# Another order of PSUM banks for the eight expansion matmuls of a slot-attention output pass

## The chip, the cores and the metric

The kernel runs on all 8 cores of one Trainium2 chip. Each core computes one element of the batch (8192 rows of 1024 numbers); the cores don't exchange anything. The metric is the device time of the slowest core in microseconds, as the median over several executions of the program.

## The reference

The input `x` is (8, 8192, 1024) in float32. The output adds two branches to it, both computed from the row-normalised `xn`:

```python
xn = _layernorm(x, axis=-1)
x = x + _L0_attn_ref(xn, ...) + _L0_ffn_ref(xn, ...)
```

The first branch is a gated recurrence over the 8192 rows, with three projections of `xn` before it and one after it (`y @ Wo + bo`). The second sends every row to its 8 best of 64 slots, collects the slots over all rows of the sequence, updates them (a recurrent cell, attention among the 64 slots, a layer norm, a projection), and gives each row its share of the slots back:

```python
slot_input = jnp.einsum('bts,btd->bsd', alpha, x)   # needs every row
...
slot_values = y @ wvp + bvp                          # 64 x 1024
out = jnp.einsum('bts,bsd->btd', alpha, slot_values)
return out @ wo + bo
```

The slots need every row before any row of the second branch's output can be made. So the rows are gone through twice.

## The kernel before

**Stages.** The kernel has three stages on each core, with the rows in 16 phases of `Tp` = 512. Pass 1 (`wo_block`, `slot_pe`, `xn_transposes`, `h_logits`, `wku_loop`, for each phase) computes the recurrence and its output, writes `x` plus the first branch to `out`, keeps the routing weights of all rows in the tile `alpha_T` (64 x 8192), and adds the slots up. The middle stage updates the 64 slots and ends in `sv_bf` (64 x 1024), the slot values. Pass 2 is what the change touches: for each phase it reads 2 MB of `out` back, adds the second branch, and writes 2 MB.

**One phase of pass 2.** Its parts are these. First the read of `out` into `prd` (L1015), one DMA of 2048 KB issued by SP. Then `zmm_phase(p2 + 1)`, which makes the expansion `z` of the next phase: for k = 0 to 7 one matmul of 64 rows by 512 columns (L992, `sv_bf` by `alpha_T`) into one bank of PSUM, which ScalarE copies as bf16 into `z_f` (L1000). Then four output tiles i = 0 to 3 of 128 rows by 1024, each 16 matmuls of 128x512 (L1031, `z_f` of this phase by `wo2_sb`) and two matmuls for the bias (L1038) into a pair of banks. VectorE adds each tile's banks to `prd` (L1046), and SP writes the tiles in two stores of 1024 KB (L1053), after the second and the fourth addition. `z_f` and `prd` have two buffers, used in turn.

**Banks.** Six banks are used, in three tensors of two: A0 and A1 in `psA`, B0 and B1 in `psB`, C0 and C1 in `psC`. The output tiles 0 to 3 use A, B, C and A again. The expansion matmul k uses `zregs[k]`. The helper `pe_claim(bank)` makes PE wait for the event that last released this bank: for an output tile that is the VectorE addition (`fadd`), for an expansion matmul it is the ScalarE copy (`zev`).

**What sets the order.** Every engine runs its own instructions in the order in which `build_walk` lists them, and waits at semaphores. PE therefore runs, for each phase: the eight expansion matmuls of the next phase, then tiles 0, 1, 2, 3. Before the first phase there are two groups of eight (`zmm_phase(0)`, `zmm_phase(1)`); the last phase, p2 = 15, has none. SP issues the read of phase p2 behind the second store of phase p2 - 1, so behind that phase's last addition. In phase p2's tile 0 VectorE waits for the read of this phase as well.

Of the kernel before, what the change touches and what calls it, by code (L numbers as in the profile page):

```python
# [104 lines left out]
def build_walk(cfg, t, P):  # L105
# [872 lines left out]
    release("A0", ("sv",))  # L978
    release("A1", ("sv",))

    zregs = ["A0", "A1", "B0", "B1", "C0", "C1", "A0", "A1"]

    def zmm_phase(q):
        if q == 0:
# [106 lines left out]
def build_nc(cfg):  # L1091
# [70 lines left out]
    with ExitStack() as ctx:  # L1162
# [121 lines left out]
        with ExitStack() as pctx:  # L1284
# [8 lines left out]
            P = Plan()  # L1293
            P.begin("dry")
            build_walk(cfg, t, P)

            with nc.Block() as block:
                @block.sync
                def _(eng):
                    P.begin("sy", eng, sems)  # L1300
                    build_walk(cfg, t, P)

                @block.gpsimd
                def _(eng):
                    P.begin("gp", eng, sems)
                    build_walk(cfg, t, P)

                @block.tensor
                def _(eng):
                    P.begin("pe", eng, sems)  # L1310
                    build_walk(cfg, t, P)

                @block.vector
                def _(eng):
                    P.begin("ve", eng, sems)
                    build_walk(cfg, t, P)

                @block.scalar
                def _(eng):
                    P.begin("se", eng, sems)  # L1320
                    build_walk(cfg, t, P)
# [73 lines left out]
```

How the kernel before makes its waits and increments, by code:

```python
    def dma(self, engine, fn, pool, event=None):  # L76
        eng_of, k = DMA_POOLS[pool]
        assert eng_of == engine
        i = self.pool_n[pool]
        self.pool_n[pool] = i + 1
        sem = f"{pool}{i % k}"
        if i >= k and self.mode == engine:
            self.eng.wait_ge(self.sems[sem], 16 * (i // k))
        return self.op(engine, fn, inc=sem, inc_n=16, event=event)
# [1 line left out]
    def wait(self, engine, event):  # L86
        if self.mode == engine:
            sem_name, val, _ = self.events[event]
            self.eng.wait_ge(self.sems[sem_name], val)
# [1 line left out]
    def wait_all_dma(self, engine, event, pool):  # L91
        if self.mode == engine:
            _, _, snap = self.events[event]
            _, k = DMA_POOLS[pool]
            for i in range(k):
                sem = f"{pool}{i}"
                if snap.get(sem, 0) > 0:
                    self.eng.wait_ge(self.sems[sem], snap[sem])
# [6 lines left out]
def build_walk(cfg, t, P):  # L105
# [972 lines left out]
        P.dma("sy", lambda s: s.dma_start(out=t.o_xnf[:], in_=t.xn_f[:]), "so")  # L1078
        P.dma("sy", lambda s: s.dma_start(out=t.o_ysbf[:], in_=t.ys_bf[:]), "so")
        P.dma("sy", lambda s: s.dma_start(out=t.o_lsb[:], in_=t.l_sb[:]), "so")
    if P.mode == "sy":
        _, k = DMA_POOLS["so"]
        n = P.pool_n["so"]
        for i in range(k):
            cnt = 16 * ((n - i - 1) // k + 1) if n > i else 0
            if cnt:
                P.eng.wait_ge(P.sems[f"so{i}"], cnt)
```

## Time and profile before

| | |
|---|---|
| median of 3 runs | 1904.35 us (1903.08 to 2004.16) |
| the profiled execution | 1903.06 us |
| span of its slowest core, core 5 | 1901.4 us |
| spans of the 8 cores | 1884.7 to 1901.4 us |
| matmul busy on core 5 | 1539.0 us of the span |
| VectorE, ScalarE busy on core 5 | 751.6 us, 569.7 us |
| pass 2 on core 5, from the first expansion matmul | from 1502.5 us to the end |
| read of `out`, from issue to landing (median) | 9.8 us |
| stores of pass 2, from issue to landing (median) | 4.9 us |

All the views below are of core 5 unless a line says otherwise, and times are counted from the start of its span. "Idle before" is the time in which an engine did nothing, and the arrow names what it waited for last. A matmul of 512 columns has a record of some 0.38 us but the next begins after 0.22 us when the granted clock is full, since they overlap; at half the clock the next begins after 0.43 us.

### The profile page before, as it was taken

How to read it: one execution, taken by the hardware profiler on the slowest of the kernel's cores; microseconds unless marked ns; L12 is line 12 of the kernel's file. 1: busy time of each engine (PE TensorE's matmuls, PEld its weight loads, DVE VectorE, ACT ScalarE, POOL GpSimd, SP SyncE). 2: the span in 40 equal slices, each digit the busy share in tenths (PEclk: the TensorE clock that was granted, in tenths of full speed). 3: DMA queues.
4: the chain of work that ended last, by engine and by line, in shares of the span. 5: the costliest groups of instructions: out<-in, count | busy, mean ns of one | idle time of the engine just before them, and what ended most of it. 6: DMA issues, size and time to landing. Idle time of an engine off the chain costs nothing.

```text
span 1901.4 us, 20893 instructions; the slowest of 8 cores (1884.7 to 1901.4 us)
## 1 busy us (share of the span) xinstructions
PE 1539.0 (81%) x7221; PEld 672.6 (35%) x7221; DVE 751.6 (40%) x1359; ACT 569.7 (30%) x926; POOL 26.6 (1%) x54
## 2 busy tenths in 40 slices
PE   0078989889899898998988989989543488888888
PEld 0034434444444443444444444444211133333332
DVE  0036446464564554635646446364302021222222
ACT  0142515325244252352532525332002111111110
POOL 0100000000000000000000000000110000000000
PEclk9999989999999999999999999999766688888888
DMA  9802020220202202112022020210596344444445
GB/s 155 179 4 75 15 89 1 89 69 21 89 13 77 89 1 89 39 51 89 1 89 60 30 89 1 89 45 1 123 170 110 89 177 177 169 158 163 164 166 199
DMA packets 42679, 166.52 MB, mean 88 GB/s; under 512 B 4290, under 2 KB 5458, under 8 KB 41682
## 3 DMA queue, kind: packets, MB, share of 16 engines
q1 hardware_dynamic: 36178, 134.29, 20.8%
q0 software_dynamic: 6400, 30.89, 9.9%
q8 instruction: 62, 1.02, 0.2%
q14 instruction: 39, 0.32, 0.1%
HBM read 128.68 MB, written 67.11 MB: 103 GB/s over the span
## 4 chain that ended last, share of the span: by engine, by line
PE 69%; DMA 10%; DVE 9%; issue 5%; ACT 4%; DVEq 3%; another core or an unknown queue 1%; ACTq 0%; POOL 0%; POOLq 0%; SPq 0%
PE psA L1031 8%; PE psA L485 6%; PE psA L489 6%; PE psC L494 6%; PE psB L494 6%; PE psC L489 6%; PE psB L485 6%; PE psA L555 4%; PE psA L347 3%; PE psC L1031 3%; PE psB L1031 3%; PE psB L555 3%; DVEq L102 3%; DMA sb_Wu_sb<-Wu_pk 2%; ACT sb_z_f L1000 2%
## 5 line engine op out<-in xcount | busy, mean ns | idle before, releaser
L19 ACT ACT_TABLE_LOAD x83 | 106.5, 1283 | 394.3 <-PE psA L555 376.6
L525 DVE SCALAR_TENSOR_TENSOR sb_a_sb<-sb_g_sb,sb_s_sb 128x512 f32<-128x512 f32 x128 | 88.7, 693 | 293.7 <-ACT sb_s_sb L510 293.7
L1031 PE MATMUL psA<-sb_wo_sb,sb_z_f 128*128 128x512 bf16 x512 | 146.5, 450 | 35.0 <-ACT sb_z_f L1000 33.3
L537 DVE TENSOR_TENSOR_SCAN sb_ys_bf<-sb_a_sb,sb_ys_bf,sb_b_sb 128x512 bf16<-128x512 f32 x120 | 154.1, 1284 | 9.7 <-issue 0.9
L347 PE MATMUL psA<-sb_Wo_sb,sb_ys_bf 128*128 128x512 bf16 x512 | 121.6, 387 | 27.2 <-DVE sb_x_sl L375 27.2
L1046 DVE TENSOR_TENSOR sb_prd<-psA,sb_prd 128x1024 f32<-128x1024 f32 x32 | 39.2, 1225 | 255.9 <-PE psA L1038 209.8
L1000 ACT ACTIVATE sb_z_f<-psA 128x512 bf16<-128x512 f32 x64 | 35.8, 631 | 307.6 <-PE psA L992 307.6
L485 PE MATMUL psA<-sb_xn_f,sb_Wp_sb 128*128 128x512 bf16 x512 | 122.5, 383 | 0.0
L489 PE MATMUL psA<-sb_xn_f,sb_Wp_sb 128*128 128x512 bf16 x512 | 121.2, 380 | 0.0
L489 PE MATMUL psC<-sb_xn_f,sb_Wp_sb 128*128 128x512 bf16 x512 | 121.0, 379 | 0.0
L485 PE MATMUL psB<-sb_xn_f,sb_Wp_sb 128*128 128x512 bf16 x512 | 120.9, 379 | 0.0
L494 PE MATMUL psB<-sb_xn_f,sb_Wu_sb 128*128 128x512 bf16 x512 | 120.9, 379 | 0.0
L494 PE MATMUL psC<-sb_xn_f,sb_Wu_sb 128*128 128x512 bf16 x512 | 120.9, 379 | 0.0
L1031 PEld LDWEIGHTS psA<-sb_wo_sb,sb_z_f 128*128 128x128 bf16 x512 | 54.7, 112 | 128.5 <-issue 93.4
L508 ACT ACTIVATE sb_g_sb<-psA,sb_bpw 128x512 f32<-128x512 f32 x64 | 44.1, 689 | 171.4 <-PE psB L494 167.5
L555 PE MATMUL psA<-sb_xn_f,sb_w1t_sb 128*128 128x512 bf16 x256 | 83.4, 497 | 12.9 <-DVE sb_xn_f L469 12.9
L460 PE MATMUL psT<-sb_ident,sb_xn_tm 128*128 128x128 bf16 x512 | 53.3, 243 | 48.1 <-DVE sb_alpha_T L425 24.0
L594 DVE MAX8 sb_m<-sb_l_sb 128x8 f32<-128x64 f32 x64 | 9.7, 213 | 195.9 <-ACT sb_l_sb L588 195.9
L508 ACT ACTIVATE sb_g_sb<-psB,sb_bpw 128x512 f32<-128x512 f32 x64 | 44.1, 689 | 130.6 <-PE psC L494 116.6
L347 PEld LDWEIGHTS psA<-sb_Wo_sb,sb_ys_bf 128*128 128x128 bf16 x512 | 49.8, 99 | 93.6 <-issue 38.6
L489 PEld LDWEIGHTS psA<-sb_xn_f,sb_Wp_sb 128*128 128x128 bf16 x512 | 50.2, 98 | 61.0 <-issue 1.0
L494 PEld LDWEIGHTS psB<-sb_xn_f,sb_Wu_sb 128*128 128x128 bf16 x512 | 50.1, 98 | 60.4
(224 smaller groups left out, 1899.9 us busy)
## 6 DMA issues: line engine op xcount, KB each, us to landing
sb_x_sl<-x SPq DMA_DIRECT2D x32, 1024.0 KB, 8.2
out<-sb_x_sl SPq DMA_DIRECT2D x32, 1024.0 KB, 4.1
sb_prd<-out SPq DMA_DIRECT2D x16, 2048.0 KB, 9.8
out<-sb_prd SPq DMA_DIRECT2D x32, 1024.0 KB, 4.9
sb_WT<-Wih_pk POOLq DMA_DIRECT2D x12, 512.0 KB, 8.7
sb_whh_pp<-Whh_pk POOLq DMA_DIRECT2D x12, 512.0 KB, 8.5
sb_Wp_sb<-Wp_pk POOLq DMA_DIRECT2D x1, 4096.0 KB, 30.4
sb_Wu_sb<-Wu_pk POOLq DMA_DIRECT2D x1, 2048.0 KB, 41.3
```

The costliest lines, as they stand in the source:

```text
L19: return eng.add_instruction(mybir.InstLoadActFuncSet(name=eng.bass.get_next_instruction_name(), act_func_set_id=idx, ins=[], outs=[]))
L102: self.eng.drain()
L347: P.op("pe", lambda e, i=i, f=f, k=k, ps=ps: e.matmul(ps[:, f * 512:(f + 1) * 512], t.ys_bf[:, k, i * 128:(i + 1) * 128], t.Wo_sb[:, k, f ...
L485: P.op("pe", lambda e, j=j, k=k, psw=psw: e.matmul(psw, t.Wp_sb[:, k, j * 128:(j + 1) * 128], t.xn_f[:, k, :], start=(k == 0), stop=(k == ...
L489: P.op("pe", lambda e, j=j, k=k, psk=psk: e.matmul(psk, t.Wp_sb[:, k, 1024 + j * 128:1024 + (j + 1) * 128], t.xn_f[:, k, :], start=(k == 0 ...
L494: P.op("pe", lambda e, j=j, k=k, psu=psu: e.matmul(psu, t.Wu_sb[:, k, j * 128:(j + 1) * 128], t.xn_f[:, k, :], start=(k == 0), stop=(k == ...
L508: P.op("se", lambda s, j=j, psw=psw: s.activation(t.g_sb[:, j % 2, :], psw, AF.Sigmoid, bias=t.bpw[:, j:j + 1]))
L525: P.op("ve", lambda v, pp=pp: v.scalar_tensor_tensor(t.a_sb[:], t.g_sb[:, pp, :], -2.0, t.s2_sb[:, pp, :], ALU.mult, ALU.mult))
L537: P.op("ve", lambda v, j=j, init=init: v.tensor_tensor_scan(t.ys_bf[:, j, :], t.a_sb[:], t.b_sb[:], init, ALU.mult, ALU.add), inc="sve", e ...
L555: P.op("pe", lambda e, jh=jh, k=k, ps=ps: e.matmul(ps, t.w1t_sb[:, k, jh * 128:(jh + 1) * 128], t.xn_f[:, k, :], start=(k == 0), stop=(k = ...
L1000: P.op("se", lambda s, k=k, q=q, ps=ps: s.activation(t.z_f[:, q % 2, k, :], ps, AF.Identity), inc="sse", event=("zev", q, k))
L1031: P.op("pe", lambda e, i=i, f=f, k=k, ps=ps, p2=p2: e.matmul(ps[:, f * 512:(f + 1) * 512], t.z_f[:, p2 % 2, k, i * 128:(i + 1) * 128], t.w ...
```

## The change

One list is replaced: the banks that the eight expansion matmuls of `zmm_phase` take in turn. Matmuls 0 and 1 go to C0 and C1 instead of A0 and A1, matmuls 4 and 5 to A0 and A1 instead of C0 and C1, and matmuls 6 and 7 to C0 and C1 instead of A0 and A1. Matmuls 2 and 3 stay in B0 and B1. The number of instructions, their order on every engine, the sizes and the DMAs are the same. Only which release each `pe_claim` waits for changes.

```diff
-    zregs = ["A0", "A1", "B0", "B1", "C0", "C1", "A0", "A1"]
+    zregs = ["C0", "C1", "B0", "B1", "A0", "A1", "C0", "C1"]
```

## Rows read from the trace of the kernel before

**Rows 1.** The page: the span in 40 slices, PE busy and granted PE clock, in tenths
```profile
PE   0078989889899898998988989989543488888888
PEclk9999989999999999999999999999766688888888
```
**Rows 2.** Chain that ended last, 1600 to 1680 us: start, duration, what
```profile
1653.26 0.55 PE psA L1038 x2
...
1653.90 1.24 DVE sb_prd L1046
...
1655.27 0.59 PE psA L992 x2
...
1660.12 4.99 PE psA L1031 x16
...
1665.64 3.56 PE psB L1031 x16
```
**Rows 3.** Timeline, 1640 to 1695 us: start, duration, engine, what, count, idle before
```profile
1649.64 3.63 PE L1031 MATMUL psA<-sb_wo_sb,sb_z_f 128*128 128x512 bf16 x16
1653.20 0.60 PE L1038 MATMUL psA<-sb_bo_tot,sb_ones_r 1*128 1x512 bf16 x2
1655.27 0.59 PE L992 MATMUL psA<-sb_alpha_T,sb_sv_bf 64*128 64x512 bf16 x2 [1.48 <-DVE sb_prd L1046]
1655.83 0.38 SPq L1015 DMA_DIRECT2D sb_prd<-out  x1
1655.83 1.09 ACT L1000 ACTIVATE sb_z_f<-psA 128x512 bf16<-128x512 f32 x2 [20.32 <-PE psA L992]
1657.76 1.12 ACT L1000 ACTIVATE sb_z_f<-psC 128x512 bf16<-128x512 f32 x2
1658.72 1.15 ACT L1000 ACTIVATE sb_z_f<-psA 128x512 bf16<-128x512 f32 x2
1660.12 4.99 PE L1031 MATMUL psA<-sb_wo_sb,sb_z_f 128*128 128x512 bf16 x16 [2.07 <-ACT sb_z_f L1000]
```
**Rows 4.** Waits, 1502 to 1902 us: engine and line, releaser, us, times, longest
```profile
DVE sb_prd L1046 <- DMA sb_prd<-out: 46.2, 4, 11.7
PE psA L1031 <- ACT sb_z_f L1000: 33.3, 15, 2.7
PE psA L992 <- DVE sb_prd L1046: 20.7, 14, 1.5
```
**Rows 5.** Timeline: the first and the last tile 0 of pass 2
```profile
1511.80 5.75 PE L1031 MATMUL psA<-sb_wo_sb,sb_z_f 128*128 128x512 bf16 x16 [1.33 <-ACT sb_z_f L1000]
1877.61 5.30 PE L1031 MATMUL psA<-sb_wo_sb,sb_z_f 128*128 128x512 bf16 x16 [1.69 <-DVE sb_prd L1046]
```
**Rows 6.** Groups by line, 1502 to 1902 us: busy us, mean ns, idle before
```profile
L1031 PE MATMUL psA<-sb_wo_sb,sb_z_f 128*128 128x512 bf16 x512 | 146.5, 450 | 35.0 <-ACT sb_z_f L1000 33.3 <-DVE sb_prd L1046 1.7
L1031 PE MATMUL psB<-sb_wo_sb,sb_z_f 128*128 128x512 bf16 x256 | 58.0, 380 | 0.0
```
**Rows 7.** Stretches: length, busy PE, PEld, DVE, ACT, POOL, PEclk, DMA share, GB/s
```profile
1656.00:1656.50 0.50, 0.50 (x3) 0.16 (x2) 0.00 (x0) 0.50 (x2) 0.00 (x0) 0.62 0.81 336
...
1662.50:1663.00 0.50, 0.50 (x2) 0.15 (x1) 0.00 (x0) 0.00 (x0) 0.00 (x0) 0.56 0.91 360
```
**Rows 8.** The same columns: two kinds of PE gap in pass 1, each twice
```profile
173.00:177.00 4.00, 2.30 (x12) 0.91 (x11) 4.00 (x7) 0.00 (x0) 0.00 (x0) 1.00 0.03 14
251.00:257.00 6.00, 3.88 (x11) 1.36 (x11) 4.25 (x8) 0.00 (x0) 0.00 (x0) 0.72 0.31 128
181.00:192.00 11.00, 7.54 (x43) 3.65 (x41) 4.76 (x12) 0.62 (x1) 0.00 (x0) 0.69 0.90 279
498.00:509.00 11.00, 7.59 (x52) 4.05 (x53) 4.33 (x12) 2.66 (x3) 0.00 (x0) 1.00 0.93 276
```
**Rows 9.** The reads of line 1015, to landing: on core 5, then on core 0
```profile
DMA to landing us min/median/max: 9.3/9.8/20.3
DMA to landing us min/median/max: 10.1/10.6/17.9
```

## The prediction

> **What bounds the kernel now.** I read the views in the order of the groups. In the strip of the page [rows 1], passes and middle stage can be told apart: PE is busy at 8 or 9 tenths in most slices up to slice 28, falls to 3 in the middle stage, and is at 8 again from slice 33. The clock line is what the reader should notice: 9 in pass 1, 8 in pass 2. So something in pass 2 makes PE lose its clock again and again.
>
> The chain of waits [rows 2] shows what. PE's bias matmuls of the last tile end, then comes a VectorE addition of 1.24 us, then the first expansion matmuls, and then ScalarE copies up to 1660.12, where tile 0 begins. Everything else in the chain is PE. The waits [rows 4] show that this is a pattern: expansion matmul 0 waits for an addition 14 times (20.7 us, 1.48 each), and tile 0 waits for ScalarE 15 times (33.3 us). The 14 are phases 1 to 14; phase 0 has nothing before it and phase 15 has no expansion. The first and the last tile 0 [rows 5] give the mean length of a phase: (1877.61 - 1511.80) / 15 = 24.39 us.
>
> So pass 2 is bound by PE and, between two phases, by a gap in which VectorE and ScalarE are the path. DMA isn't: VectorE waits for the read of `out` in 4 phases [rows 4], but this doesn't reach PE, which works on tile 1 meanwhile.
>
> **The gap before.** I take the one at 1653 [rows 3]. The bias pair begins at 1653.20; such a pair keeps PE for 0.53 us (tile 0 ends at 1660.12 + 4.99 = 1665.11 and tile 1 starts at 1665.64, with a pair between them [rows 2]), so PE is free at 1653.73. Tile 3's addition releases A0 and A1 and matmul 0 starts at 1655.27. ScalarE starts 0.56 us later, at 1655.83, and its eight copies end at 1658.72 + 1.15 = 1659.87. Tile 0 starts 0.25 us after that, at 1660.12. The gap is 6.39 us. Matmuls 6 and 7, on A0 and A1, are copied last, and tile 0 needs exactly these banks: it waits for all eight copies.
>
> **The change, part by part.**
>
> 1. *Matmuls 0 and 1 on C0 and C1.* These were released by tile 2's addition, which runs during tile 3, so matmul 0 follows the bias pair at 1653.73 and not at 1655.27: the copies start 1.54 us earlier, at 1654.29. Matmuls 2 and 3 (B0, B1) follow at once. ScalarE's other wait there, that `z_f`'s buffer is free, is for the end of tile 3, which is past.
> 2. *Matmuls 4 and 5 on A0 and A1.* They now bear the wait for tile 3's addition and start at 1655.27, ready for ScalarE at 1655.83. Queued behind them on PE are matmuls 6 and 7 and tile 0, which is late anyway. ScalarE comes to its fifth copy at 1654.29 + (1657.76 - 1655.83) = 1656.22. The cover is 0.39 us, so this wait costs nothing; if the cover goes, the cost is the excess.
> 3. *Matmuls 6 and 7 on C0 and C1.* They need copies 0 and 1, long done. Tile 0 needs only the sixth copy, which ends at 1657.76 + 1.12 = 1658.88 in the old timing, 0.99 us before the eighth. Copies 7 and 8 run beside tile 0; tile 2 wants their banks some 8 us later.
>
> Sum for one gap: 1.54 + 0.99 = 2.53 us. Tile 0 starts at 1657.59 and the gap is 3.86 us. Over 14 gaps this is 35.4 us. At the start of pass 2, where sixteen copies run in a row, only the 0.99 counts. Phase 15 keeps its wait for tile 3's addition (1.69 us) [rows 5]. Together 36.4 us.
>
> 4. *The clock.* In the gap of the rows the granted clock fell to 0.50, the 1.2 GHz level, at about 1656.1 and was back at 2.4 GHz at about 1662.9 [rows 7]. The part in tile 0, 2.8 us at half speed, costs 1.4 us: tile 0 took 4.99 us, a full-speed tile 3.56 [rows 2]. Over pass 2, `psA` is busy 146.5 us in 32 tiles, and `psB` 58.0 in 16, or 3.63 each [rows 6]: 146.5 - 32 x 3.63 = 30.3 us are lost to the slow clock in 16 tiles 0, some 1.9 each. The clock fell in every one of the 15 gaps.
>
> Does it still fall in a gap of 3.86 us? In it PE's records would show two pauses, about 0.5 us ahead of matmul 4 and 1.3 us ahead of tile 0, against 1.48 and 2.07 now [rows 3]. Pass 1 has the nearest gaps [rows 8]. A single pause of 1.70 us before a tile (the stretch at 173) left the clock at 1.00, one of 2.12 us (at 251) didn't; it fell at 2 of 15 such places. The stretch with transposes, PE busy 7.5 of 11 us, ended either way: 0.69 at 181, 1.00 at 498, with a fall at 11 of 15 boundaries. The new gap lies between the two kinds, so I take a fall in half of the gaps, 7 of 14. When it falls, more of the slow stretch lies in tile 0, since tile 0 begins 2.53 us earlier: (1662.9 - 1657.59) / 2 = 2.7 us a fall. That is 7 x 2.7 = 18.9 us where 14 x 1.9 = 26.6 were: 7.7 us back. Bounds: no fall gives 26.6 back; a fall in every gap costs 14 x 2.7 - 26.6 = 11.2 more.
>
> The Trainium skill ("TensorE: Matmul & The Clock Gate", section "Why this matters for your kernels") warns only of longer pauses between bursts than any of the two in this gap, before or after. By that rule the clock would stay up and the whole 26.6 us would come back; but it speaks against the trace, where pauses as short as 1.48 and 2.07 us lost it 15 times of 15, so it is a rival and not the forecast.
>
> 5. *The read of `out`.* It is issued 0.7 us after the last addition (1655.83 against 1653.90 + 1.24), as now, and lands 9.8 us later, at 1665.6; on core 0 it takes 10.6 [rows 9]. Tile 0's banks are ready at 1665.6 now and will be at 1657.59 + 3.56 + 0.53 = 1661.7, or 1664.4 with a slow clock, so VectorE will wait for the read in nearly every phase. PE does not, until tile 3 wants A0 and A1. The loop is: issue 0.7, landing L, addition 1.23, release 0.13, tile 3 up to its addition 1653.90 - 1649.64 = 4.26, addition 1.23: L + 7.6 us. With L = 9.8 it is 17.4, with 10.6 it is 18.2, against a phase of 24.39 - 2.53 - 1.9 = 19.96 us even if no clock is lost. It costs nothing until L passes 12.3.
>
> **Sum.** 36.4 + 7.7 = 44.1 us off the profiled execution's 1903.06 gives 1859. The median of the runs is 1.3 us above that execution; I leave the forecast at 1859, against 1904.35.
>
> **The rivals.**
>
> - *The clock never falls* (the page's rule): 36.4 + 26.6 = 63 us, 1840. For it: the single pauses of 1.7 us that left it up. Against: the expansion matmuls fill only part of the gap and use half of the rows.
> - *The clock falls in every gap*: 36.4 - 11.2 = 25 us, 1878. For it: 15 of 15 now. Against: the gap shrinks from 6.39 to 3.86 us and each pause with it.
> - *The read becomes the bound.* Phases are shorter, so the same 4 MB come more often, and the other cores ask more often too. At L = 15 a phase is 22.6 us: (24.39 - 22.6) x 14 = 25 us, 1878. Against it: the medians of L are 9.8 and 10.6 now, the lowest 9.3 and 10.1 [rows 9], so the bulk is near the bottom.
> - *Slower than before*, by the same loop: only once L + 7.6 passes 24.39, at L over 16.8. At L = 18 a phase is 25.6 us, 14 x 1.2 = 17 us more, 1920. One read did take 20.3 us [rows 9], but the median says that the others don't come near.
> - *The order of banks does nothing*, since the copies turn out to be held by something else: 1903. Against: ScalarE's idle time ahead of the copies ends with the matmul [rows 3].
>
> **How the numbers follow.** Forecast 0.60 (its own range 1850 to 1869), clock never falls 0.13, clock always falls 0.14, read as the bound 0.06, no effect 0.04, slower 0.03. The likeliest gives 1859. For 8 in 10 I reach most of the way to the two clock cases: 1842 to 1877. About 2% is what a measurement of this kernel can tell from no change; 2% faster is 1866. The forecast's range lies below that with 0.55 of its 0.60; with 0.13 for the clock that stays and 0.03 of the read's case, faster has 0.71. The rest of the forecast, the clock that always falls, no effect and the rest of the read's case give 0.25 for within 2%. Slower has 0.04.
>
> **What would show it.** In the waits, the one of an expansion matmul for the addition stays 14 times but falls from 1.48 to about 0.5 us, and lies behind the first four matmuls. Tile 0 starts about 3.9 us after the bias pair. The wait of tile 0 for ScalarE falls from 33.3 us to some 20. The read is what ends VectorE's wait in nearly all phases, with no wait of tile 3's matmuls for it. The busy time of `psA` falls from 146.5 to about 139 us. Pass 1 and the middle stage don't change. I am wrong if tile 3 waits for VectorE, if ScalarE stands idle ahead of its fifth copy, or if the slow clock takes much more or less than half of the gaps.

## The result and the profile after

The changed kernel takes 1858.36 us in the median of 8 runs, the kernel before 1903.29 us in the runs beside them. The ratio is 0.9771, with a 95% interval of 0.9759 to 0.9784: faster by 2.3%, 44.9 us. The forecast was 1859. In some executions, whatever the kernel, the cores of one die show a lower granted clock and take some per cent longer; ratios compare the others alone, and the four kernels whose ratio would have a wide interval or none (`e9_spread_ahead`, `e10_early_fill`, `e11_six_fill`, `e12_readahead`) are read by the phase lengths in their traces.

The spans of the profiled execution (1861.40 us) are 1844.0 to 1859.9 us over the eight cores; the slowest is again core 5. All that follows is of core 5 unless it says otherwise. First the timeline around one gap, where [rows 3] showed the same of before (start, duration, engine, what, count, idle before):

```profile
1639.22 0.60 PE L1038 MATMUL psA<-sb_bo_tot,sb_ones_r 1*128 1x512 bf16 x2
1639.75 0.60 PE L992 MATMUL psC<-sb_alpha_T,sb_sv_bf 64*128 64x512 bf16 x2
1639.93 1.22 DVE L1046 TENSOR_TENSOR sb_prd<-psA,sb_prd 128x1024 f32<-128x1024 f32 x1 [2.87 <-PE psA L1038]
1640.20 0.59 PE L992 MATMUL psB<-sb_alpha_T,sb_sv_bf 64*128 64x512 bf16 x2
1640.33 1.08 ACT L1000 ACTIVATE sb_z_f<-psC 128x512 bf16<-128x512 f32 x2 [16.20 <-PE psC L992]
1641.30 0.59 PE L992 MATMUL psA<-sb_alpha_T,sb_sv_bf 64*128 64x512 bf16 x2 [0.51 <-DVE sb_prd L1046]
...
1642.25 1.12 ACT L1000 ACTIVATE sb_z_f<-psA 128x512 bf16<-128x512 f32 x2
1643.21 1.14 ACT L1000 ACTIVATE sb_z_f<-psC 128x512 bf16<-128x512 f32 x2
...
1643.67 6.26 PE L1031 MATMUL psA<-sb_wo_sb,sb_z_f 128*128 128x512 bf16 x16 [1.35 <-ACT sb_z_f L1000]
```

The reader is to see three things. The expansion matmul on C0 follows the bias pair at once, 0.53 us after its start, ahead of VectorE's addition and not behind it. The wait for that addition has moved to the matmul on A0 at 1641.30 and is 0.51 us long. And tile 0 starts at 1643.67, while ScalarE is still at copies 7 and 8 (1643.21 + 1.14 = 1644.35). From 1639.75, when the bias pair frees PE, the gap is 3.92 us; it was 6.39. Over the 14 gaps of core 5 the mean is 3.88 us; it was 6.41.

The waits of pass 2 (engine and line, releaser, us, times, longest) against [rows 4]:

```profile
DVE sb_prd L1046 <- DMA sb_prd<-out: 163.7, 15, 11.9
...
PE psA L1031 <- ACT sb_z_f L1000: 18.6, 15, 1.4
```

And the groups by line (busy us, mean ns, idle before) against [rows 6]:

```profile
L1031 PE MATMUL psA<-sb_wo_sb,sb_z_f 128*128 128x512 bf16 x512 | 140.7, 437 | 20.3 <-ACT sb_z_f L1000 18.6 <-DVE sb_prd L1046 1.7
L992 PE MATMUL psA<-sb_alpha_T,sb_sv_bf 64*128 64x512 bf16 x32 | 10.3, 404 | 7.2 <-DVE sb_prd L1046 7.2
```

VectorE now waits for the read of `out` in 15 phases, not 4, and none of this reaches PE: tiles 1 to 3 have no idle time in front of them. PE's wait for VectorE ahead of the expansion fell from 20.7 us to 7.2 us, tile 0's wait for ScalarE from 33.3 to 18.6, and the busy time of `psA` from 146.5 to 140.7. That last one is the clock. Three tiles 0 in a row, from the timeline:

```profile
1643.67 6.26 PE L1031 MATMUL psA<-sb_wo_sb,sb_z_f 128*128 128x512 bf16 x16 [1.35 <-ACT sb_z_f L1000]
...
1666.54 5.08 PE L1031 MATMUL psA<-sb_wo_sb,sb_z_f 128*128 128x512 bf16 x16 [1.30 <-ACT sb_z_f L1000]
...
1688.24 3.61 PE L1031 MATMUL psA<-sb_wo_sb,sb_z_f 128*128 128x512 bf16 x16 [1.30 <-ACT sb_z_f L1000]
```

The record of a tile at full clock is 3.61 to 3.63 us long. So one tile 0 lost 2.6 us, the next 1.4 and the third nothing, behind the same gap of 3.9 us. This pattern of three repeats through most of pass 2. On core 5, 10 of the 14 tiles 0 behind a changed gap lost time, 20.8 us together, and 4 did not; on the other cores 8 to 10 of 14 did. Before, it was 14 of 14, and 26.6 us.

### The profile page after: what moved, and what is told of

Its sections match the earlier page's. It is cut to its first block, busy times and chain, and to the rows that moved or that the text cites. A ratio compares the mean times of both kernels' runs of the same rounds, so it can differ in the third digit from the quotient of the medians.

```text
span 1859.9 us, 20893 instructions; the slowest of 8 cores (1844.0 to 1859.9 us)
## 1 busy us (share of the span) xinstructions
PE 1520.4 (82%) x7221; PEld 668.2 (36%) x7221; DVE 751.2 (40%) x1359; ACT 568.6 (31%) x926; POOL 26.6 (1%) x54
## 4 chain that ended last, share of the span: by engine, by line
PE 69%; DMA 10%; DVE 9%; issue 5%; DVEq 3%; ACT 2%; another core or an unknown queue 1%; ACTq 0%; POOL 0%; POOLq 0%; SPq 0%
PE psA L1031 8%; PE psA L485 6%; PE psC L494 6%; PE psA L489 6%; PE psC L489 6%; PE psB L494 6%; PE psB L485 6%; PE psA L555 4%; PE psA L347 3%; PE psC L1031 3%; PE psB L1031 3%; PE psB L555 3%; DVEq L102 3%; DMA sb_Wu_sb<-Wu_pk 2%; DMA sb_WT<-Wih_pk 2%
## 5 line engine op out<-in xcount | busy, mean ns | idle before, releaser
L1031 PE MATMUL psA<-sb_wo_sb,sb_z_f 128*128 128x512 bf16 x512 | 140.7, 437 | 20.3 <-ACT sb_z_f L1000 18.6
L1046 DVE TENSOR_TENSOR sb_prd<-psA,sb_prd 128x1024 f32<-128x1024 f32 x32 | 39.2, 1225 | 249.6 <-DMA sb_prd<-out 163.7
L1000 ACT ACTIVATE sb_z_f<-psC 128x512 bf16<-128x512 f32 x64 | 35.6, 627 | 268.7 <-PE psC L992 268.7
L494 PEld LDWEIGHTS psC<-sb_xn_f,sb_Wu_sb 128*128 128x128 bf16 x512 | 50.1, 98 | 60.4
## 6 DMA issues: line engine op xcount, KB each, us to landing
sb_prd<-out SPq DMA_DIRECT2D x16, 2048.0 KB, 10.6
sb_Wu_sb<-Wu_pk POOLq DMA_DIRECT2D x1, 2048.0 KB, 41.6
```

Source lines behind the costliest of these rows:

```text
L494: P.op("pe", lambda e, j=j, k=k, psu=psu: e.matmul(psu, t.Wu_sb[:, k, j * 128:(j + 1) * 128], t.xn_f[:, k, :], start=(k == 0), stop=(k == ...
L1031: P.op("pe", lambda e, i=i, f=f, k=k, ps=ps, p2=p2: e.matmul(ps[:, f * 512:(f + 1) * 512], t.z_f[:, p2 % 2, k, i * 128:(i + 1) * 128], t.w ...
```

## The experiments

All of them are edits of pass 2. Where a phase length is given, it is the distance between the same instruction in successive phases, in the steady part of pass 2.

### The two parts of the change, each alone

`e1_early` keeps the early start but puts A0 and A1 last, so tile 0 still needs all eight copies. `e2_six` keeps the late start but has A0 and A1 at places 4 and 5, so tile 0 needs six.

```diff
-    zregs = ["C0", "C1", "B0", "B1", "A0", "A1", "C0", "C1"]
+    zregs = ["C0", "C1", "B0", "B1", "C0", "C1", "A0", "A1"]   # e1_early
+    zregs = ["A0", "A1", "B0", "B1", "A0", "A1", "C0", "C1"]   # e2_six
```

> Banks C0 C1 B0 B1 C0 C1 A0 A1: only the start of the copies moves, tile 0 still needs all eight copies. Theory (two additive parts, 1.54 and 0.99 us a gap): the gap from the bias pair to tile 0 is 6.4 - 1.5 = 4.9 us; 14 x 1.54 = 21.6 us off, of which the slow clock takes some 5 us back since it still falls in most gaps: about 1886. Rival (the early start is all of the gain, the copies 7 and 8 are hidden anyway): as the changed kernel, 1858.

> Banks A0 A1 B0 B1 A0 A1 C0 C1: the first matmul still waits for the last addition, but tile 0 needs only six copies. Theory: the gap is 6.4 - 1.0 = 5.4 us; 15 x 0.99 = 15 us off, some 5 taken back by the slow clock, which falls in every gap: about 1893. Rival (tile 0 is held by PE's own order and not by the copies): no change, 1903.

Measured: `e1_early` has a ratio to before of 0.9947 (0.9930 to 0.9964), about 10 us faster; `e2_six` 0.9930 (0.9909 to 0.9952), about 13 us. I expected 17 and 10. One by one the two parts give 10 + 13 = 23 us, and together 44.9. The timeline of `e1_early`, core 2:

```profile
1655.40 6.29 PE L1031 MATMUL psA<-sb_wo_sb,sb_z_f 128*128 128x512 bf16 x16 [2.24 <-ACT sb_z_f L1000]
...
1679.29 6.30 PE L1031 MATMUL psA<-sb_wo_sb,sb_z_f 128*128 128x512 bf16 x16 [2.24 <-ACT sb_z_f L1000]
```

A phase is 23.89 us. The bias pair before the second of these tiles 0 ends at 1674.44, where the expansion begins, so the gap is 4.85 us, 1.54 shorter than before, as expected. But the 14 tiles 0 of this core now take 6.1 to 6.3 us each, where they took 5.0 to 6.5. `psA` is busy for 155.4 us, against 146.5 before: the slow clock took 9 us of the 21.6 back. In `e2_six` the gap is 5.41 us, 0.98 shorter than before, and the phases settle at 23.9 us as well, with 2.1 us lost in each tile 0 (core 2):

```profile
1671.30 5.74 PE L1031 MATMUL psA<-sb_wo_sb,sb_z_f 128*128 128x512 bf16 x16 [0.63 <-ACT sb_z_f L1000]
...
1695.19 5.75 PE L1031 MATMUL psA<-sb_wo_sb,sb_z_f 128*128 128x512 bf16 x16 [0.63 <-ACT sb_z_f L1000]
```

So the gap of each kernel is the one expected, and my charge of 5 us for the clock was too small in `e1_early`. Gap and loss add up to the same in both, 4.85 + 2.7 and 5.41 + 2.1 us, so the clock came back at the same place behind the bias pair. Why it did, no run here tells.

### The same with the clock held up

To take the clock out, PE gets idle work in its pauses: transposes of the identity into a PSUM bank that nobody reads in pass 2. `e3_fill_new` does this on the changed kernel, `e4_fill_old` on the kernel before, `e10_early_fill` and `e11_six_fill` on the two halves.

```diff
+    def fill(n):
+        for _ in range(n):
+            P.op("pe", lambda e: e.transpose(t.psT0[:, 0:128], t.ident[:], t.ident[:]))
...
+            if q >= 2 and k == 4:
+                fill(8)          # old banks: 22 ahead of k == 0
             pe_claim(reg)
...
+        if q >= 2:
+            fill(20)             # old banks: 42
```

> The changed kernel plus idle work for PE in its two pauses: 8 transposes of 128x128 ahead of expansion matmul 4 and 20 behind matmul 7, in 14 phases, into a bank that nobody reads. Theory: the granted clock stays at 1.00 through the gaps, the busy time of psA falls from 140.7 to about 119, and the kernel gains some 22 us: 1836. The gap itself keeps its 3.9 us. Rival (the fall doesn't depend on PE's work in the gap, or the transposes don't hold the clock): 1858 or, if they push tile 0 back, up to 10 us more.

> The kernel before plus the same idle work in its pauses: 22 transposes ahead of matmul 0, 42 behind matmul 7, in 14 phases. Theory: the clock stays up, psA's busy time falls from 146.5 to about 119, 28 us off: 1875. With the run of the changed kernel with idle work this gives the effect of the order of banks at a constant clock, 14 x 2.53 + 1 = 36 us. Rival (order and clock can't be told apart, the bank order works by the clock alone): both runs with idle work give the same time.

> Banks C0 C1 B0 B1 C0 C1 A0 A1 (early start, eight copies) plus idle work for PE in the pauses: 6 transposes ahead of matmul 4, 38 behind matmul 7. Theory (the two parts of the change add up at a constant clock, and only the slow clock ate the single ones): a phase is 22.74 - 1.54 = 21.2 us, and 14 x 1.54 = 21.6 us come off the old banks with idle work: ratio to before about 0.974. Rival (the parts need each other): 22.5 us a phase or more.

> Banks A0 A1 B0 B1 A0 A1 C0 C1 (late start, six copies) plus idle work: 22 transposes ahead of matmul 0, 6 ahead of matmul 4, 20 behind matmul 7. Theory: a phase is 22.74 - 0.99 = 21.75 us, 15 us off the old banks with idle work: ratio to before about 0.978. Rival as above: 22.5 us a phase or more.

Measured: `e3_fill_new` 0.9672 (0.9654 to 0.9689), `e4_fill_old` 0.9855 (0.9834 to 0.9876). The stretch of pass 2 in both (length, busy PE, PEld, DVE, ACT, POOL, granted clock, DMA share, GB/s), first the new banks (core 1), then the old ones (core 4):

```profile
1510.00:1840.00 330.00, 317.11 (x1657) 133.94 (x1656) 76.04 (x64) 57.53 (x115) 0.00 (x0) 0.99 0.59 198
```
```profile
1510.00:1870.00 360.00, 348.01 (x2160) 163.42 (x2160) 78.28 (x64) 57.26 (x114) 0.00 (x0) 0.99 0.50 179
```

The granted clock is 0.99 in both, where the kernel before has 0.85 and the changed kernel 0.91 over the same stage (core 5, in this order):

```profile
1512.00:1901.00 389.00, 329.04 (x1264) 120.52 (x1262) 78.31 (x64) 56.44 (x112) 0.00 (x0) 0.85 0.45 168
```
```profile
1512.00:1860.00 348.00, 315.03 (x1264) 117.05 (x1261) 77.83 (x64) 56.54 (x113) 0.00 (x0) 0.91 0.56 187
```

`psA` is busy 117.6 and 119.4 us in the two kernels with idle work. By ratio they take 1841 and 1876 us; I expected 1836 and 1875. Both expectations of the theory hold: the clock follows what PE does in the gap, and the order of banks has a worth of its own. Between the two, 0.9855 - 0.9672 = 0.0183 of 1902 us is 35 us, against the 36.4 of the sum.

The timelines give it per phase, since on nearly all cores each phase of these kernels behind the first is as long as the next. Core 1 of `e3_fill_new` is an exception, with four phases that are 0.3 to 0.6 us longer; there the read of `out` takes 12.0 us in the median, and tile 3 has to wait for VectorE. The bias pairs of tile 3 follow each other in `e4_fill_old` (core 4) by 22.74 us and in `e3_fill_new` (core 1) by 20.23 us:

```profile
1665.31 0.60 PE L1049 MATMUL psA<-sb_bo_tot,sb_ones_r 1*128 1x512 bf16 x2
...
1688.05 0.60 PE L1049 MATMUL psA<-sb_bo_tot,sb_ones_r 1*128 1x512 bf16 x2
```
```profile
1650.17 0.60 PE L1049 MATMUL psA<-sb_bo_tot,sb_ones_r 1*128 1x512 bf16 x2
...
1670.40 0.60 PE L1049 MATMUL psA<-sb_bo_tot,sb_ones_r 1*128 1x512 bf16 x2
...
1708.19 3.61 PE L1042 MATMUL psA<-sb_wo_sb,sb_z_f 128*128 128x512 bf16 x16 [0.53 <-DVE sb_prd L1057]
```

The halves, `e10_early_fill` (core 0) first and `e11_six_fill` (core 0) second, by the starts of tile 3:

```profile
1652.83 3.63 PE L1042 MATMUL psA<-sb_wo_sb,sb_z_f 128*128 128x512 bf16 x16
...
1674.04 3.63 PE L1042 MATMUL psA<-sb_wo_sb,sb_z_f 128*128 128x512 bf16 x16
```
```profile
1649.86 3.63 PE L1042 MATMUL psA<-sb_wo_sb,sb_z_f 128*128 128x512 bf16 x16
...
1671.62 3.63 PE L1042 MATMUL psA<-sb_wo_sb,sb_z_f 128*128 128x512 bf16 x16
```

| banks, clock held up | phase, us | shorter by | the sum said |
|---|---|---|---|
| old | 22.74 | | |
| early start, eight copies | 21.21 | 1.53 | 1.54 |
| late start, six copies | 21.76 | 0.98 | 0.99 |
| both, the change | 20.23 | 2.51 | 2.53 |

At a constant clock the two parts add up. Only the slow clock makes them look as though they needed each other. The ratio of `e10_early_fill`, 0.974 as expected, has a wide interval (0.958 to 0.990), and `e11_six_fill` has none; the phase lengths carry this reading.

### A shorter chain still

`e5_four` gives A0 and A1 to matmuls 2 and 3, so tile 0 needs only four copies.

```diff
-    zregs = ["C0", "C1", "B0", "B1", "A0", "A1", "C0", "C1"]
+    zregs = ["C0", "C1", "A0", "A1", "B0", "B1", "C0", "C1"]
```

> Banks C0 C1 A0 A1 B0 B1 C0 C1: tile 0 needs only four copies, but matmul 2 is now the one that waits for the last addition. Theory: matmul 2 starts 1.54 us behind the bias pair, its copy 0.56 later at 2.1 us, which is 0.5 us after the second copy could end, so ScalarE stands idle once; copies 3 and 4 end at 3.2 us and tile 0 starts at 3.45 us, against 3.92 in the changed kernel. 14 x 0.47 = 7 us off and a little more by the clock: 1850. Rival (the cover of the matmul that waits was already used up, so a shorter chain gives nothing): 1858 or slower.

Measured: 0.9751 (0.9736 to 0.9766), against 0.9771 for the change; in time some 4 us less, and the intervals overlap. Core 6:

```profile
1679.18 0.59 PE L992 MATMUL psA<-sb_alpha_T,sb_sv_bf 64*128 64x512 bf16 x2 [0.94 <-DVE sb_prd L1046]
...
1680.99 5.22 PE L1031 MATMUL psA<-sb_wo_sb,sb_z_f 128*128 128x512 bf16 x16 [0.35 <-ACT sb_z_f L1000]
```

The expansion began at 1677.63, so this gap is 3.36 us where I expected 3.45. ScalarE does stand idle once, ahead of its third copy:

```profile
1679.65 1.09 ACT L1000 ACTIVATE sb_z_f<-psA 128x512 bf16<-128x512 f32 x2 [0.36 <-PE psA L992]
```

But in 11 to 13 of the 14 gaps a tile 0 still lost time to the clock, more often than in the change, whose gap is longer. The pause in the middle is longer (0.94 against 0.51 us) and the one ahead of tile 0 shorter (0.35 against 1.35). The losses are smaller on average than in the change, and their sum is about the same: 16 to 23 us a core against 17 to 21. Nor are all the gaps 3.36 us; some are 3.7 to 4.2, and the mean of a core is 3.46 to 3.66 us, where the change has 3.87 to 4.04. By the gap shown 14 x (3.92 - 3.36) = 7.8 us were to be had; about half of it came. The longer gaps took part of the rest, and the clock, which I had expected to add to the gain, added nothing.

### When the read of `out` is late

Two kernels queue one more read ahead of each read of `out`, of 2 MB and of 4 MB, into a buffer that nobody reads.

```diff
+        if p2 >= 1:
+            P.dma("sy", lambda s, p2=p2: s.dma_start(
+                out=t.xtra[:, 0:4, :],   # 4 MB: 0:8, from (p2 - 1) * Tp
+                in_=t.i_x[p2 * Tp:p2 * Tp + 4 * 128, :]...), "sx")
```

> The changed kernel with one more read of 2 MB (of x, into a buffer nobody reads) queued ahead of each read of out in phases 1 to 15. Theory (a phase can't be shorter than L + 7.6 us, L the time from the issue of the extra read to the landing of the read of out): L becomes 14.5 to 16, the bound 22 to 23.6 against a mean phase of 21.6; 15 x (0.5 to 2) = 8 to 30 us slower than the changed kernel: 1866 to 1888. Tile 3 then waits for VectorE. Rival (the read is hidden anyway, VectorE's wait never reaches PE): 1858.

> The same with an extra read of 4 MB. Theory: L is 20 to 22 us, a phase 27.6 to 29.6, 15 x 6 to 15 x 8 = 90 to 120 us slower than the changed kernel: 1948 to 1978, the last addition's wait for A0 and A1 in the chain of each phase. Rival (the read is hidden): 1858. This is the mechanism by which the change could have been slower than before.

Measured: 1.0127 (1.0095 to 1.0159) and 1.0718 (1.0684 to 1.0752), so (1.0127 - 0.9771) x 1903 = 68 us and likewise 180 us more than the changed kernel. Direction and place are right, the size is not: I expected 8 to 30 and 90 to 120. The read of `out` lands 16.6 us after its issue in the first kernel (median, core 4) and 22.7 us in the second (core 6):

```profile
DMA to landing us min/median/max: 14.0/16.6/21.2
DMA to landing us min/median/max: 20.0/22.7/24.3
```

This gives L + 7.6 = 24.2 and 30.3, but the phases of these cores are 26.5 and 33.1 us long. The timeline of the second shows what the formula left out:

```profile
1645.92 0.60 PE L1043 MATMUL psC<-sb_bo_tot,sb_ones_r 1*128 1x512 bf16 x2
1655.44 6.11 PE L1036 MATMUL psA<-sb_wo_sb,sb_z_f 128*128 128x512 bf16 x16 [8.92 <-DVE sb_prd L1051]
1661.49 0.60 PE L1043 MATMUL psA<-sb_bo_tot,sb_ones_r 1*128 1x512 bf16 x2
```

Tile 3 waits 8.92 us for the addition that frees A0 and A1, and then runs 6.11 us and not 3.63: the wait costs the clock too, in the very loop that is the bound. The loss is 2.5 us here, 1.3 to 2.9 and in the mean 2.2 us over the phases of this core, and 1.9 in the mean on core 4 of the first kernel. With it, 30.3 + 2.2 = 32.5 and 24.2 + 1.9 = 26.1 us; the 0.4 to 0.6 us that are left stay open. The rest of the expectation holds: the read reaches PE through tile 3's banks and through nothing else (139.6 us of waits of `psA` for the addition, in 15 phases).

The other direction, the changed kernel with the read of phase p2 + 1 issued ahead of the stores of phase p2:

```diff
-        P.dma("sy", ... out=t.prd[:, pr, :, :] ..., event=("pread", p2))
+        if p2 == 0:
+            pread(0)
+        if p2 + 1 < NPH:
+            pread(p2 + 1)
```

> The changed kernel with the read of out issued one phase earlier and nothing else. VectorE's waits for the read (163.7 us in 15 phases) should vanish. Theory (they never reached PE, since the loop through the read is 3 us or so shorter than a phase): same time as the changed kernel, 1858, ratio 0.977. Rival (the read was on the path in some phases): 1850 or less.

Measured: mostly phases of 20.2, 21.7 and 22.9 us as in the changed kernel, a mean of 21.4 to 21.8 us on the cores (21.5 to 21.9 there), and times from 1856.89 us; the ratio, 0.9733, has a wide interval (0.9610 to 0.9857) that holds the changed kernel's. VectorE's waits for the read are gone from the trace, 163.7 us of them on the changed kernel's core 5, and nothing was gained. They were beside the path.

### No gap at all

`e8_spread` issues the expansion in pairs behind the output tiles, in the two banks of the transposes, and lets the output tiles take A, B and C in turn across phases. `e9_spread_ahead` adds the early read.

```diff
+        trio = [("A0", "A1", t.psA), ("B0", "B1", t.psB), ("C0", "C1", t.psC)]
+        oregs = [trio[(4 * p2 + i) % 3] for i in range(4)]
...
             release(r1, ("fadd", p2, i))
+            if p2 + 1 < NPH:
+                zmm_phase(p2 + 1, (2 * i, 2 * i + 1))
```

> No gap at all: the eight expansion matmuls of the next phase are issued in pairs behind the output tiles 0 to 3 and use the two PSUM banks of the transposes (free in pass 2), and the output tiles take A, B and C in turn through all phases. Theory: a phase is 4 x 4.09 + 8 x 0.22 = 18.1 us of PE's work with the clock at 1.00, if the read allows it: L + 7.6 with L = 10 to 11 gives 17.6 to 18.6. 15 x (21.6 - 18.4) = 48 us off the changed kernel and some 5 at the start: about 1806. Rival (PE isn't the bound once the gap is gone, since copies and additions share the banks' ports or the read is late): 1825 or more, with PE idle ahead of tile 3.

> The spread kernel with the read of out issued one phase earlier: SP issues the read of phase p2 + 1 ahead of the stores of phase p2, so it has a whole phase to land. Theory (what lengthened single phases of the spread kernel from 18.5 to 19 or 21 us was a late read that held tile 3): every phase is 18.5 us (4 x (4.09 + 0.53)) on every core, and the kernel gains another 5 to 15 us: about 1808. Rival (the long phases come from elsewhere, and the read ahead only meets the stores): no change, 1820, or slower.

Measured: `e8_spread` 0.9623 (0.9604 to 0.9643), 1816.33 us at best, with spans of 1799.2 to 1814.8. It is the fastest kernel with a ratio, but it is not as fast as expected: 0.9623 x 1903 is 1831 us, and I had said 1806. The timeline on core 3:

```profile
1648.96 3.63 PE L1029 MATMUL psA<-sb_wo_sb,sb_z_f 128*128 128x512 bf16 x16
1652.52 0.60 PE L1036 MATMUL psA<-sb_bo_tot,sb_ones_r 1*128 1x512 bf16 x2
1653.05 0.60 PE L992 MATMUL psT<-sb_alpha_T,sb_sv_bf 64*128 64x512 bf16 x2
1653.59 3.63 PE L1029 MATMUL psB<-sb_wo_sb,sb_z_f 128*128 128x512 bf16 x16
```

There is no idle time of PE left in such a phase, the granted clock of this core is 1.00 over pass 2, and the pair costs 0.53 us, not 2 x 0.22 as I expected: 4 x (4.09 + 0.53) = 18.5 us, which is the phase length. But single phases took 19 to 21.7 us. On core 5:

```profile
1720.86 5.30 PE L1029 MATMUL psC<-sb_wo_sb,sb_z_f 128*128 128x512 bf16 x16 [1.26 <-DVE sb_prd L1044]
...
1741.62 3.61 PE L1029 MATMUL psA<-sb_wo_sb,sb_z_f 128*128 128x512 bf16 x16 [0.51 <-DVE sb_prd L1044]
```

Here, with phases of 18.5 us, the read does reach tile 3. With the early read every phase in the steady part of `e9_spread_ahead` is 18.5 us on all eight cores, and its spans are 1793.9 to 1811.3 us. Its lowest time was 1812.80 us. So the late read is what made those phases long. In the profiled execution it cost some 3.5 us (1816.33 against 1812.80), in the three others of `e8_spread`, of 1824 to 1833 us, more. It matters little before the gap is gone. The few microseconds between these 1812.80 us and the 1808 expected stay open.

## Why the prediction was right

**The gap.** The step said 6.39 to 3.86 us; it became 3.92 in the gap shown and went from 6.41 to 3.88 in the mean of 14. Its two terms, 1.54 and 0.99 us, were measured one by one at a constant clock as 1.53 and 0.98. The start of pass 2, where only the second counts, was 9.32 us from the first expansion matmul (1502.48) to tile 0 (1511.80), and is 1511.46 - 1503.12 = 8.34 now.

**The cover of the matmul that waits.** The second part gave 0.39 us of cover between the matmul on A0 being ready and ScalarE coming to it. The fifth copy started at 1642.25, and 1641.30 + 0.56 = 1641.86: 0.39. `e5_four` shows the other side, where the wait stands two places earlier and ScalarE is held for 0.36 us.

**The clock.** The likeliest case held, that it falls in some gaps and not in others. Both factors were off, in opposite directions: I said 7 falls of 14 at 2.7 us, 18.9 us; on core 5 there were 10, of 2.6 to 2.9 and of 1.4 to 1.6 us, together 20.8. One error lies in taking the slow stretch of one gap as that of all, the other in the half, which was a choice between two kinds of gap and no more. That they nearly cancel is luck. By the busy time of `psA` the whole of pass 2 lost 140.7 - 116.2 = 24.5 us against 30.3 before, 5.8 back where I had 7.7. The rival in which it never falls is what `e3_fill_new` makes by force: I gave 1840 us for it, and by its ratio it takes 1841. The rule of the Trainium skill ("TensorE: Matmul & The Clock Gate", section "Why this matters for your kernels") that led to this rival warns only of longer pauses between bursts of matmuls than any here. By it the clock would have stayed up, and it did not: the longest pause in the new gap is 1.35 us, and the clock still fell in 8 to 10 of 14. The rival in which it always falls gave 1878, outside of what was measured.

**The sum.** On core 5: 14 x 2.53 + 1.0 for the gaps, and 5.8 by the clock, is 42.2 us, less 0.6 because pass 2 began later in the second trace (1503.12 against 1502.48): 41.6. The spans differ by 1901.4 - 1859.9 = 41.5. The medians differ by 44.9, and I had 44.1. The slowest core's span is a little less improved than the medians; nothing in the trace explains these 3 us, and they are of the size by which runs of one kernel differ. So the sum is confirmed to some 2 us, the clock's part, and that the forecast meets the median to within 1 us is luck.

**The read.** It has the form that I gave it, an idle time of VectorE in nearly all phases that does not reach PE; `e12_readahead` shows that its worth is nil. The bound L + 7.6 was too low by 2.3 to 2.8 us where it decides, mostly because it left out the clock that the wait itself costs. So the rival "slower than before" begins sooner than at the L of 16.8 that I gave. `e6_read2mb` shows where: its cores 0 to 3, with medians of L of 15.2 and 15.3, have spans of 1886.5 to 1898.7 us, as long as the cores of before (1884.7 to 1901.4), and core 4, with 16.6, has 1925.1. With the change's own L of 10.6 it makes no difference. A smaller slip: the phase without a loss is 20.23 us, as `e3_fill_new` has it, and not 19.96, since the mean of 24.39 takes in the last, shorter gap, which has no expansion.

**The chances.** No effect is out: the interval ends at 0.9784.

## What to carry to other kernels

Where two kinds of work share PSUM banks, write down for each claim which release it waits for and how long ago that was. The banks that are wanted next should be emptied early, and the ones released last should be claimed late. Here these are the same two banks, A0 and A1, so the two rules pull against each other: with A0 and A1 claimed first the gap is 5.41 us (`e2_six`), claimed last 4.85 (`e1_early`), and claimed behind just enough other work to hide the wait 3.88. A gap on PE can cost twice, once as idle time and once by the clock behind it (6.4 and 1.9 us here), so price both, and measure them apart by giving PE idle work in the gap. When a gap closes, look again at the transfers that were beside the path: the read of `out` was worth nothing with phases of 21.6 us, 0.3 to 0.6 us in a few phases of one core with phases of 20.2, and up to 3 us in single phases where 18.5 was possible.

## What the runs showed of the hardware

The transposes held the clock. 28 transposes of 128x128 in a gap of 3.9 us kept the granted clock at 0.99 over pass 2, and 64 of them did so in a gap of 6.4 us; without them it was 0.91 and 0.85. The Trainium skill ("TensorE: Matmul & The Clock Gate", section "Part 4: PE-mode transpose") says that transposes don't bring PE to its full clock, since they don't count as a busy PE in the same way; in these two runs they kept it there. Whether transposes alone would raise it, no run here shows.

The eight expansion matmuls, which use 64 of 128 rows, did not hold it when they stood together: in the changed kernel PE's records cover 3.92 - 0.51 - 1.35 = 2.06 us of the gap, and the clock fell behind it more often than not. In `e5_four` the gap was shorter, 3.36 us, with pauses of 0.94 and 0.35 us, and it fell in 11 to 13 of 14. In `e8_spread` the same matmuls stood in pairs between the output tiles, with no pause, and the granted clock of core 3 was 1.00 over pass 2. Which of the two counts, the pauses or the rows in use, no run here tells apart.

A pair of expansion matmuls costs 0.54 us ahead of a group of 128-row matmuls (1653.05 to 1653.59 in `e8_spread`) and 0.45 within a run of its own kind (1639.75 to 1640.20 above).
